# A fused attention and mixture-of-experts kernel: where the first silus and four halves of the shared expert stand at the end of the attention

## The chip, the cores and the metric

One Trainium2 chip, of which the kernel uses one core. The time is that of the program on the device, in microseconds. The kernel before was timed three times; their median counts. One more execution was taken by the hardware profiler, and all rows below come from it. TensorE is PE in the rows, VectorE DVE, ScalarE ACT, GpSimd POOL, SyncE SP.

## What is computed

Two layers over 2 x 2048 tokens of 256 channels, in float32:

```python
x = L0_attn_X
x = x + _L0_attn_ref(_layernorm(x), Wq, Wv, q_norm_w, v_norm_w)
x = x + _L0_ffn_ref(_layernorm(x), Wg, W1, W2, W3, Ws1, Ws2, Ws3)

# attention: no softmax, a running sum of outer products
K = X.reshape(B, L, H, d)                      # H = 16 heads of d = 16
Q = rms_norm_multihead((X @ Wq.T).reshape(B, L, H, d), q_norm_w)
V = rms_norm_multihead((X @ Wv.T).reshape(B, L, H, d), v_norm_w)
W = jnp.cumsum(jnp.einsum('blhd,blhde->blhde', K, V), axis=1)
out = jnp.einsum('blhd,blhde->blhe', Q, W)

# feed-forward: top 4 of 32 experts, and a shared expert of 256 hidden columns
scores = softmax(xf @ Wg); weights, indices = top_k(scores, 4)
y[tok] += (silu(xg @ W1[e]) * (xg @ W3[e]) @ W2[e]) * w     # for each expert e
z = silu(xf @ Ws1) * (xf @ Ws3) @ Ws2
return y + z
```

## The kernel before

The tokens are 32 tiles of 128 (NT = 32). Each engine has its own program, written out in Python and tied to the others by counting semaphores. Three stages follow each other:

1. The attention, with the routing woven in. `pipelined(NT, depth, step)` runs a step function that does parts of up to ten tiles in one step, each part for the tile `tile_of(skew)`. TensorE transposes, projects, makes the scores and the outputs; a tile's normalised second input (x2) is transposed 5 steps behind its first part and kept in x2T_all. Routing works on pairs of tiles (`closing(...)` is the second tile of a pair): router logits transposed (lgT, 5 steps behind), logits (6 behind, `pT0[:, P:P+2E]`, copied by ScalarE to lg), on VectorE the top four, the mask and the running count mcum, on TensorE the rank matmuls (7 behind, L846 and L847), copied by ScalarE to rk, and from it on VectorE the places posi. GpSimd scatters each tile's rows to the experts' table xs in memory by four indirect DMAs (L467).
2. Between attention and experts. TensorE counts the rows of each expert (L897), VectorE makes from it the table of 144 blocks (a chain of small operations, `tab(...)`, L1284 to L1329), TensorE turns two results into rows (L914, L916), VectorE writes them as brow and erow. SyncE waits for all scatters and for brow, then loads the blocks' rows into xg (L389).
3. The experts: 144 blocks of 128 rows. In a block TensorE transposes the rows (L946), ScalarE copies them (L647), TensorE multiplies by W1 and W3 (L967), ScalarE and VectorE do silu and product, TensorE multiplies by W2 (L985), ScalarE scales, GpSimd scatters to ys. After that the four parts of each token are summed and written out.

The shared expert is done in 8 groups g of 512 tokens. `shared_half(g, m, n)` is one of its four hidden halves (m: which 128 of 256 hidden columns; n = 0 the silu side, n = 1 the gate side), two matmuls of 128x512 (L741). `h_bank(g, m, n)` says in which PSUM bank it lies; banks come free from other work at different times, which sets the places of the halves. `half_silu(g, m)` (L624, ScalarE), `half_gate(g, m)` (L1249, VectorE: silu times gate side, into gsh), `shared_z(g)` (L757, TensorE: four output tiles, by turns in banks pQV and pO) and `add_z(t)` (L1259, VectorE, adds an output tile to x) make the rest. Groups 0 to 2 (NPRE = 3) are done before the blocks; five halves of groups 0 and 1 stand within the last steps of the attention, the others after them:

```python
if (a := closing(tile_of(7))) is not None:      # TensorE, the rank matmuls
    wait(pe, S["mask_done"], a.p + 1)
    wait(pe, S["mcum_done"], 2 * a.p + 1)
...
for q in range(QT):                             # TensorE, shared_z(g)
    wait(pe, S["z_done"], min(QT * g + q - 1, QT * LATE))
```

The last line is the one that ties an output tile to the adds: output q of a group waits until all but the one before it are added. VectorE's two gates of group 0 and the others of groups 0 and 1 stand at written places among the `tab(...)` operations, the four adds of group 0 behind L1317 among the last of them. Silu is in another table set of ScalarE than the exp and log of the attention, so `preload_act_table(ACT.Silu)` (L619) stands once, after the attention's last step. Of group 3 the two halves of m = 0 are done before and within the first block: H(3,0,0) ahead of the blocks, H(3,0,1) between the transposes of blocks 0 and 1; its silu and its product (kept) are done at block 1.

Of the kernel before, what the change touches and what calls it, by code (L numbers as in the profile page):

```python
# [12 lines left out]
ALU = mybir.AluOpType  # L13
ACT = mybir.ActivationFunctionType
# [37 lines left out]
def build(nc, X, Wq, Wv, q_norm_w, v_norm_w, Wg, W1, W2, W3, Ws1, Ws2, Ws3, out):  # L52
# [30 lines left out]
    ZC = 32  # L83
# [34 lines left out]
    with ctx:  # L118
# [386 lines left out]
        def _(act):  # L505
# [12 lines left out]

            normalise(0)
# [9 lines left out]
            def step(tile_of):  # L529
# [47 lines left out]
                if (a := closing(tile_of(7))) is not None:  # L577
                    wait(act, S["logits_ps"], a.p + 1)
                    wait(act, S["mask_done"], a.p - 1)
                    wait(act, S["max_done"], 2 * (a.p - 1))  # L580
                    act.copy(lg[:, a.pb].rearrange("p h e -> p (h e)"), pT0[:, P:P + 2 * E]).then_inc(S["lg_done"], 1)
                if (a := closing(tile_of(6))) is not None:
                    wait(act, S["lgT_ps"], a.p + 1)
                    wait(act, S["logits_ps"], a.p)
                    act.copy(lgT[:], pT0[:, 0:P]).then_inc(S["lgT_done"], 1)
                if (a := tile_of(0)) is not None and a.t > 1:
                    normalise(a.t)
# [33 lines left out]
            def half_silu(g, m):  # L621
                wait(act, S["h_ps"], FC * g + m + 1)
                wait(act, S["gsh_done"], FC * (g - 1) + m + 1)
                act.activation(sg[:, m, :], h_bank(g, m, 0)[:], ACT.Silu).then_inc(S["silu_done"], 1)  # L624

            def shared_silu(g):
                for m in range(FC):
                    half_silu(g, m)

            for g in range(NPRE):  # L630
                shared_silu(g)

# [8 lines left out]
            def expert_step(tile_of):  # L641
                if (a := tile_of(0)) is not None:
                    if a.t == 1:
                        half_silu(NPRE, 0)
                    wait(act, S["xT_ps"], a.t + 1)
                    wait(act, S["hb_ps"], a.t - 1)
                    act.copy(xgT[:, a.b], (pT0, pQV)[a.b][:, 0:D].rearrange("p (g m) -> p g m", g=KC)).then_inc(S["xT_done"], 1)  # L647
# [73 lines left out]
        def _(pe):  # L721
# [39 lines left out]
            def step(tile_of):  # L761
# [68 lines left out]
                if (a := closing(tile_of(6))) is not None:  # L830
                    if a.t == NT - 1:
                        pe.wait_ge(S["x2_done"], NT)
                        shared_half(1, 0, 1)
                    wait(pe, S["lgT_done"], a.p + 1)
                    wait(pe, S["x2T_done"], a.t + 2, NT)
                    wait(pe, S["qT_done"], a.t + 6, NT)
                    wait(pe, S["qm_done"], a.t + 6, NT)
                    pe.matmul(pT0[:, P:P + 2 * E], lgT[:], pick, start=True, stop=True).then_inc(S["logits_ps"], 1)
                if (a := closing(tile_of(7))) is not None:
# [54 lines left out]

            pe.wait_ge(S["mcum_done"], NT)
# [3 lines left out]
            pe.wait_ge(S["x2T_done"], NT)  # L899
            pe.wait_ge(S["silu_done"], 1)  # L900
            shared_half(1, 1, 1)
            pe.wait_ge(S["silu_done"], 2)
            shared_half(2, 0, 0)
            pe.wait_ge(S["gsh_done"], 1)
            shared_half(2, 0, 1)
# [34 lines left out]
            def expert_step(tile_of):  # L940
                if (a := tile_of(0)) is not None:
# [6 lines left out]
                    if a.t == 0:  # L948
                        shared_half(NPRE, 0, 1)
# [37 lines left out]
            shared_half(NPRE, 0, 0)  # L987
            pipelined(NJ, 4, expert_step)
# [20 lines left out]
        def _(dve):  # L1009
# [75 lines left out]

            def mask_scores(a, j):
                wait(dve, S["scores_ps"], 4 * a.t + j + 1)
                wait(dve, S["o_ps"], a.t)
                dve.tensor_tensor(s_sb[:, j].rearrange("p g r l -> p (g r) l"), pS[j][:].rearrange("p (n l) -> p n l", l=P),  # L1089
                                  tri[:].unsqueeze(1).to_broadcast([P, 4, P]), ALU.mult).then_inc(S["masked"], 1)  # L1090

            def step(tile_of):
# [21 lines left out]
                if (a := closing(tile_of(8))) is not None:  # L1114
# [4 lines left out]
                                      ).then_inc(S["mcum_done"], 1)  # L1119
                if (a := tile_of(3)) is not None:  # L1120
                    mask_scores(a, 3)
# [124 lines left out]
            def half_gate(g, m):  # L1246
                wait(dve, S["silu_done"], FC * g + m + 1)
                wait(dve, S["z_ps"], QT * (g - 1))
                dve.tensor_tensor(gsh[:, g % 2, m, :], sg[:, m, :], h_bank(g, m, 1)[:], ALU.mult).then_inc(S["gsh_done"], 1)  # L1249

            def shared_gate(g):
                for m in range(FC):
                    half_gate(g, m)

# [35 lines left out]
            dve.wait_ge(S["ys_zeroed"], 16 * ZC)  # L1290
            half_gate(0, 0)
            half_gate(0, 1)
# [7 lines left out]
            half_gate(1, 0)  # L1300
# [53 lines left out]
            shared_add(2)  # L1354
            dve.wait_ge(S["w2_in"], 16)

            def expert_step(tile_of):
# [4 lines left out]
                if (a := tile_of(0)) is not None:  # L1363
                    if a.t == 1:
                        dve.wait_ge(S["silu_done"], FC * NPRE + 1)
                        dve.tensor_tensor(sg[:, 0, :], sg[:, 0, :], h_bank(NPRE, 0, 1)[:], ALU.mult).then_inc(S["kept"], 1)
# [110 lines left out]
```

## Time and profile before

| | us |
|---|---|
| three runs | 560.71, 558.83, 557.15 |
| median | 558.83 |
| profiled execution | 559.33 |
| its span, first to last instruction | 557.4 |
| TensorE busy | 527.4 (95%) |
| VectorE busy | 382.2 (69%) |
| ScalarE busy | 376.5 (68%) |
| GpSimd busy | 331.8 (60%) |
| mean granted TensorE clock | 0.983 of full |

### The profile page before, as it was taken

What the parts mean: (1) busy time and instruction counts of PE and PEld (TensorE: products, weight loads), DVE (VectorE), ACT (ScalarE), POOL (GpSimd) and SP (SyncE); (2) the same over time, 40 slices, a digit from 0 to 9 for tenths busy, and PEclk for the clock granted to TensorE, in tenths of its full rate; (3) what the DMA queues carried; (4) which work ended last, traced back from release to release, by engine and by line L of the source; (5) the groups of instructions that cost most, each with busy time, mean ns of one, the idle gap of its engine ahead of it and who ended that gap; (6) DMA issues with size and microseconds to landing.
All of it is one profiled execution on the core that took longest, in us unless ns stands there. A gap on an engine that the chain in (4) does not pass through costs nothing.

```text
span 557.4 us, 18176 instructions
## 1 busy us (share of the span) xinstructions
PE 527.4 (95%) x5177; PEld 383.1 (69%) x5177; DVE 382.2 (69%) x1354; ACT 376.5 (68%) x1258; POOL 331.8 (60%) x367
## 2 busy tenths in 40 slices
PE   6798999999999999699999999999999999997996
PEld 2355666666666665357998988999999995544554
DVE  7698999999999996664444444444444446744786
ACT  2687899988989985402766766777677776653452
POOL 6010377776777777771665555666666564446992
PEclk8999999999999999899999999999999999998999
DMA  8998355556456554954676776766666554428999
GB/s 259 316 292 264 125 217 211 187 215 227 186 198 246 188 192 152 366 194 127 195 219 201 221 225 199 214 193 194 194 193 198 180 187 145 143 79 342 408 409 347
DMA packets 65088, 123.29 MB, mean 221 GB/s; under 512 B 9824, under 2 KB 44000, under 8 KB 64992
## 3 DMA queue, kind: packets, MB, share of 16 engines
q1 hardware_dynamic: 47824, 78.07, 44.1%
q0 software_dynamic: 13056, 39.86, 19.2%
q10 hardware_dynamic: 4112, 4.19, 2.3%
q8 instruction: 45, 0.74, 0.6%
q14 instruction: 51, 0.42, 0.3%
HBM read 58.49 MB, written 63.60 MB: 219 GB/s over the span
## 4 chain that ended last, share of the span: by engine, by line
PE 79%; DMA 5%; DVE 4%; issue 4%; ACT 3%; POOL 2%; SPq 1%; ACTq 1%; DVEq 0%; POOLq 0%
PE pS L967 18%; PE pQV L828 10%; PE pS L985 9%; PE pS L741 8%; PE pS L795 5%; PE pO L888 5%; DMA xg<-xs 3%; PE pO L869 3%; PE pT L946 3%; PE pQV L946 2%; PE pQV L757 2%; PE pO L757 2%; PE pT L774 2%; PE pO L803 2%; PE pT L817 1%
## 5 line engine op out<-in xcount | busy, mean ns | idle before, releaser
L495 POOL DMA_INDIRECT ys<-gsh,dst x144 | 138.1, 959 | 108.3 <-ACT gsh L663 86.6
L467 POOL DMA_INDIRECT xs<-xg,posi x128 | 123.8, 967 | 52.1 <-issue 31.4
L967 PE MATMUL pS<-after_a,x2T_all 128*128 128x128 f32 x1024 | 135.5, 276 | 0.0
L967 PEld LDWEIGHTS pS<-after_a,x2T_all 128*128 128x128 f32 x1024 | 124.5, 192 | 0.0
L1375 DVE TENSOR_TENSOR after_a<-after_a,pS 128x128 f32<-128x128 f32 x144 | 41.5, 288 | 79.9 <-ACT after_a L651 76.1
L1346 DVE COPY x2T_all<-w 128x512 f32 x144 | 63.9, 444 | 32.9 <-issue 32.5
L985 PE MATMUL pS<-w,after_a 128*128 x256 | 76.7, 381 | 0.0
L1089 DVE TENSOR_TENSOR w<-pS,tri 128x512 f32<-128x512 f32 x96 | 65.1, 679 | 1.0 <-PE pS L795 1.0
L828 PE MATMUL pQV<-w 128*128 128x512 f32 x128 | 63.7, 621 | 0.5 <-ACT w L533 0.5
L663 ACT ACTIVATE gsh<-pS,xg 128x256 f32<-128x256 f32 x128 | 60.6, 474 | 0.4 <-issue 0.4
L662 ACT CAST dst<-xg 128x1 int32 x128 | 24.5, 191 | 45.3 <-PE pS L985 43.3
L741 PE MATMUL pS<-x2T_all,ws 128*128 128x512 f32 x104 | 50.6, 636 | 1.3 <-ACT sg L624 0.7
L651 ACT ACTIVATE after_a<-pS 128x128 f32<-128x128 f32 x144 | 40.1, 279 | 16.5 <-PE pS L967 10.7
L482 POOL TENSOR_SCALAR_AFFINE_SELECT w<-w 128x512 f32<-128x512 f32 x32 | 20.6, 643 | 43.3 <-ACT w L527 43.0
L500 POOL TENSOR_TENSOR w<-w 128x512 f32<-128x512 f32 x32 | 40.7, 1272 | 7.7 <-DMA w<-ys 7.4
L985 PEld LDWEIGHTS pS<-w,after_a 128*128 128x128 f32 x256 | 38.9, 192 | 0.4 <-issue 0.4
L556 ACT ACTIVATE w<-pT,mwq 128x128 f32<-128x128 f32 x128 | 36.8, 379 | 1.9 <-PE pT L817 1.7
L741 PEld LDWEIGHTS pS<-x2T_all,ws 128*128 128x128 f32 x104 | 20.9, 207 | 24.6 <-issue 24.3
L795 PE MATMUL pS<-w 32*128 32x256 f32 x512 | 36.7, 401 | 0.0
L828 PEld LDWEIGHTS pQV<-w 128*128 128x128 f32 x128 | 22.2, 194 | 20.2 <-issue 18.2
L888 PE MATMUL pO<-w 128*32 128x128 f32 x1024 | 34.6, 274 | 1.3 <-POOL w L482 0.6
L647 ACT COPY after_a<-pT 128x256 f32<-128x256 f32 x72 | 26.1, 363 | 11.4 <-PE pT L946 11.3
(221 smaller groups left out, 1019.8 us busy)
## 6 DMA issues: line engine op xcount, KB each, us to landing
xg<-xs SPq DMA_DIRECT2D x128, 160.0 KB, 2.8
ys<-gsh SPq DMA_DIRECT2D x32, 512.0 KB
w<-ys SPq DMA_DIRECT2D x32, 512.0 KB, 15.3
w<-in_L_ffn_W ACTq DMA_DIRECT2D x1, 4096.0 KB, 18.6
out<-xall SPq DMA_DIRECT2D x14, 256.0 KB, 7.2
xs<-padrow SPq DMA_DIRECT2D x32, 80.0 KB
xg<-xs SPq DMA_DIRECT2D x32, 80.0 KB, 2.2
ys<-gsh,dst POOLq DMA_INDIRECT x144
```

Source lines behind the costliest of these rows:

```text
L467: pool.indirect_dma_start(out=xs, out_offset=bass.IndirectOffsetOnAxis(ap=posi[:, a.r8, k:k + 1], axis=0), in_=xr[:, a.r8, :], in_offset=N ...
L495: pool.indirect_dma_start(out=ys, out_offset=bass.IndirectOffsetOnAxis(ap=dst[:, j % 8:j % 8 + 1], axis=0), in_=y[:, j % 8, :], in_offset= ...
L663: act.activation(y[:, a.r8, :], pS[2 + a.b][:, 0:D], ACT.Copy, scale=xg[:, a.r8, bass.ds(e[0] + D, 1)]).then_inc(S["y_done"], 1)
L741: last = pe.matmul(h_bank(g, m, n)[:], ws13[:, k, n, m * P:(m + 1) * P], x2T_all[:, k, g * TG:(g + 1) * TG], start=(k == 0), stop=(k == KC ...
L795: last = pe.matmul(pS[j][:, g * 256:(g + 1) * 256], xnT[32 * j:32 * j + 32, a.r3, g, :], qm[32 * j:32 * j + 32, :, g, :], start=(g == 0), ...
L828: last = pe.matmul(pQV[:], xnT[:, a.r3, k, :], wqv[:, k, :], start=(k == 0), stop=(k == KC - 1))
L888: last = pe.matmul(pO[32 * j:32 * j + 32, g * P:(g + 1) * P], vp[:, a.b, 4 * g + j, r:r + 2, :], s_sb[:, j, g, r, :], start=False, stop=(r ...
L967: last = pe.matmul(pS[a.b][:, n * P:(n + 1) * P], w13_staged(a.t)[:, (2 * k + n) * F:(2 * k + n + 1) * F], xgT[:, a.b, k, :], start=(k == ...
L985: last = pe.matmul(pS[2 + a.b][:, 0:D], geT[:, a.b, :], w2_of(e), start=True, stop=True)
L1089: dve.tensor_tensor(s_sb[:, j].rearrange("p g r l -> p (g r) l"), pS[j][:].rearrange("p (n l) -> p n l", l=P), tri[:].unsqueeze(1).to_broa ...
L1346: dve.tensor_copy(w13_staged(j), w13[:, bass.ds(staged_of(j), 1), :, :, :].rearrange("p a k n f -> p (a k n f)")).then_inc(S["w13_staged"], 1)
L1375: dve.tensor_tensor((ge if mixed(a.t) else geT)[:, a.b, :], sge[:, a.b, :], pS[a.b][:, F:2 * F], ALU.mult).then_inc(S["ge_done"], 1)
```

## The change

Three things are moved; no computation is added or left out but two loads of activation tables.

- ScalarE loads the silu table behind the last lgT copy (step 6 behind, last tile), does both silus of group 0 there, goes on to the copy of the last logits, and loads the exp and log set again for what is left of the attention. The silu load after the attention stays.
- TensorE does H(1,1,1) and H(2,0,0) behind the last logits matmul and ahead of the last rank matmuls, and H(2,0,1) ahead of the count. VectorE does the two gates of group 0 behind its last first-half count (mcum), ahead of the rest of the last pair's routing, and the first gate of group 1 takes the old place of group 0's gates in the tables.
- Of group 3, H(3,0,1) follows H(3,0,0) ahead of block 0; its silu on ScalarE stands ahead of the blocks, its product on VectorE behind group 2's adds and ahead of the stage copy of block 1.

```diff
@@ ScalarE
                     act.copy(lg[:, a.pb].rearrange("p h e -> p (h e)"), pT0[:, P:P + 2 * E]).then_inc(S["lg_done"], 1)
+                    if a.t == NT - 1:
+                        act.preload_act_table_set("natural_log_exp_and_others")
                 if (a := closing(tile_of(6))) is not None:
                     ...
                     act.copy(lgT[:], pT0[:, 0:P]).then_inc(S["lgT_done"], 1)
+                    if a.t == NT - 1:
+                        act.preload_act_table(ACT.Silu)
+                        shared_silu(0)
...
             act.preload_act_table(ACT.Silu)
...
-            for g in range(NPRE):
+            for g in range(1, NPRE):
                 shared_silu(g)
+            half_silu(NPRE, 0)
...
                 if (a := tile_of(0)) is not None:
-                    if a.t == 1:
-                        half_silu(NPRE, 0)
@@ TensorE
                     pe.matmul(pT0[:, P:P + 2 * E], lgT[:], pick, start=True, stop=True).then_inc(S["logits_ps"], 1)
+                    if a.t == NT - 1:
+                        pe.wait_ge(S["x2T_done"], NT)
+                        pe.wait_ge(S["silu_done"], 1)
+                        shared_half(1, 1, 1)
+                        pe.wait_ge(S["silu_done"], 2)
+                        shared_half(2, 0, 0)
...
+            pe.wait_ge(S["gsh_done"], 1)
+            shared_half(2, 0, 1)
             pe.wait_ge(S["mcum_done"], NT)
             pe.wait_ge(S["rk_done"], NP2)
             pe.matmul(pT0[:, 0:E], ones16[:], mcum[:, 0, 0, :], start=True, stop=True).then_inc(S["cnt_ps"], 1)
-            pe.wait_ge(S["x2T_done"], NT)
-            pe.wait_ge(S["silu_done"], 1)
-            shared_half(1, 1, 1)
-            pe.wait_ge(S["silu_done"], 2)
-            shared_half(2, 0, 0)
-            pe.wait_ge(S["gsh_done"], 1)
-            shared_half(2, 0, 1)
...
-                    if a.t == 0:
-                        shared_half(NPRE, 0, 1)
...
             shared_half(NPRE, 0, 0)
+            shared_half(NPRE, 0, 1)
             pipelined(NJ, 4, expert_step)
@@ VectorE
                     dve.tensor_tensor(mcum[:, a.pb, 1, :], mcum[:, a.pb, 0, :], mask[:, a.pb, 0, :], ALU.add
                                       ).then_inc(S["mcum_done"], 1)
+                    if a.t == NT - 1:
+                        dve.wait_ge(S["ys_zeroed"], 16 * ZC)
+                        shared_gate(0)
...
-            dve.wait_ge(S["ys_zeroed"], 16 * ZC)
-            half_gate(0, 0)
-            half_gate(0, 1)
+            half_gate(1, 0)
...
-            half_gate(1, 0)
...
             shared_add(2)
+            dve.wait_ge(S["silu_done"], FC * NPRE + 1)
+            dve.tensor_tensor(sg[:, 0, :], sg[:, 0, :], h_bank(NPRE, 0, 1)[:], ALU.mult).then_inc(S["kept"], 1)
             dve.wait_ge(S["w2_in"], 16)
...
-                if (a := tile_of(0)) is not None:
-                    if a.t == 1:
-                        dve.wait_ge(S["silu_done"], FC * NPRE + 1)
-                        dve.tensor_tensor(sg[:, 0, :], sg[:, 0, :], h_bank(NPRE, 0, 1)[:], ALU.mult).then_inc(S["kept"], 1)
```

TensorE at the end of the attention before the change, from the last logits matmul on. L846 and L847 are the rank matmuls, L897 the count, L741 the halves by their banks (pS0 is H(1,1,1), pS2 H(2,0,0), pS1 H(2,0,1), pS3 H(2,1,0)), L757 the outputs of group 0:

```order
L838 MATMUL pT0<-after_a 128x64
L846 MATMUL pT0<-mask,tri16 128x64
L847 MATMUL pT0<-mcum,ones16 128x64
L897 MATMUL pT0<-mcum,ones16 128x32
L741 MATMUL pS0<-x2T_all,ws13 128x512 x2
L741 MATMUL pS2<-x2T_all,ws13 128x512 x2
L741 MATMUL pS1<-x2T_all,ws13 128x512 x2
L741 MATMUL pS3<-x2T_all,ws13 128x512 x2
L757 MATMUL pQV<-ws2,gsh 128x256 x2
L757 MATMUL pO<-ws2,gsh 128x256 x2
```

The same place after it (L842 is the last logits matmul, L856 and L857 rank, L909 the count, L745 the halves, L761 the outputs):

```order
L842 MATMUL pT0<-after_a 128x64
L745 MATMUL pS0<-x2T_all,ws13 128x512 x2
L745 MATMUL pS2<-x2T_all,ws13 128x512 x2
L856 MATMUL pT0<-mask,tri16 128x64
L857 MATMUL pT0<-mcum,ones16 128x64
L745 MATMUL pS1<-x2T_all,ws13 128x512 x2
L909 MATMUL pT0<-mcum,ones16 128x32
L745 MATMUL pS3<-x2T_all,ws13 128x512 x2
L761 MATMUL pQV<-ws2,gsh 128x256 x2
L761 MATMUL pO<-ws2,gsh 128x256 x2
```

Two halves now stand ahead of rank and a third ahead of the count. The order of all that follows the count is as it was.

VectorE where the tables begin, before the change: L1282 stands behind all routing, L1284 is the first operation that needs the count, L1249 are the two gates of group 0 (by their gate side's bank, pS1 and pS3):

```order
L1282 TENSOR_SCALAR padrow<-padrow 128x32
L1284 TENSOR_TENSOR pad_f<-pT0,ecap 128x32
L1285 CAST pad_i<-pad_f 128x32
L1286 TENSOR_TENSOR after_a<-pad_f,ebase 128x32
L1288 TENSOR_SCALAR after_a<-after_a 128x32
L1289 TENSOR_SCALAR after_a<-after_a 128x32
L1249 TENSOR_TENSOR gsh<-sg,pS1 128x512
L1249 TENSOR_TENSOR gsh<-sg,pS3 128x512
L1293 TENSOR_SCALAR after_a<-after_a 128x32
```

The same place after it (L1291 needs the count, L1093 with pO is the first gate of group 1):

```order
L1289 TENSOR_SCALAR padrow<-padrow 128x32
L1291 TENSOR_TENSOR pad_f<-pT0,ecap 128x32
L1292 CAST pad_i<-pad_f 128x32
L1293 TENSOR_TENSOR after_a<-pad_f,ebase 128x32
L1295 TENSOR_SCALAR after_a<-after_a 128x32
L1296 TENSOR_SCALAR after_a<-after_a 128x32
L1093 TENSOR_TENSOR gsh<-sg,pO 128x512
L1298 TENSOR_SCALAR after_a<-after_a 128x32
```

The gates of group 0 now come earlier, behind the last pair's first mcum (L1131), ahead of the reciprocal (L1154) and the rest of that pair's routing; one gate of group 1 has their place:

```order
L1131 TENSOR_TENSOR mcum<-mcum,mask 128x32
L1093 TENSOR_TENSOR gsh<-sg,pS1 128x512
L1093 TENSOR_TENSOR gsh<-sg,pS3 128x512
L1154 RECIPROCAL rin<-se 128x2
L1177 TENSOR_TENSOR vm<-mask,rk 128x64
```

They stood seven operations into the tables and stand before them now; the order of the tables themselves is unchanged.

## Rows read from the trace of the kernel before

**Rows 1.** The page's part 4, the chain that ended last: shares of the span.

```profile
PE 79%; DMA 5%; DVE 4%; issue 4%; ACT 3%; POOL 2%; SPq 1%; ACTq 1%; DVEq 0%; POOLq 0%
```

**Rows 2.** Timeline of TensorE: start, us, instruction, count, [idle before it <- what ended it].

```profile
227.96 0.33 PE L838 MATMUL pT<-after_a 128*128 128x64 f32 x2
...
230.11 0.19 PE L846 MATMUL pT<-mask,tri 128*128 128x64 f16 x1 [1.82 <-DVE mcum L1118]
...
231.74 0.21 PE L897 MATMUL pT<-mcum,ones 128*128 128x32 f16 x1 [1.41 <-DVE mcum L1096]
232.63 9.89 PE L741 MATMUL pS<-x2T_all,ws 128*128 128x512 f32 x16 [0.69 <-ACT sg L624]
242.36 1.03 PE L757 MATMUL pQV<-ws,gsh 128*128 128x256 f32 x4
...
245.81 1.88 PE L741 MATMUL pT<-x2T_all,ws 128*128 128x512 f32 x4
247.62 0.60 PE L914 MATMUL pT<-ident,ejc 128*1 128x128 f32 x4
...
251.09 1.13 PE L757 MATMUL pQV<-ws,gsh 128*128 128x256 f32 x4 [0.51 <-DVE xall L1259]
...
257.14 1.96 PE L741 MATMUL pS<-x2T_all,ws 128*128 128x512 f32 x4 [0.61 <-DVE xall L1259]
258.93 0.38 PE L946 MATMUL pT<-ident,xg 128*128 128x128 f32 x2
259.15 1.88 PE L741 MATMUL pS<-x2T_all,ws 128*128 128x512 f32 x4
...
261.09 1.06 PE L967 MATMUL pS<-after_a,x2T_all 128*128 128x128 f32 x8
```

**Rows 3.** Timeline of ScalarE, same columns.

```profile
226.43 0.27 ACT L585 COPY after_a<-pT 128x128 f32<-128x128 f32 x1
228.33 0.21 ACT L581 COPY lg<-pT 128x64 f32<-128x64 f32 x1 [1.63 <-PE pT L838]
...
230.59 1.28 ACT L619 ACT_TABLE_LOAD   x1
231.89 1.09 ACT L624 ACTIVATE sg<-pS 128x512 f32<-128x512 f32 x2
...
261.07 0.60 ACT L624 ACTIVATE sg<-pS 128x512 f32<-128x512 f32 x1 [1.29 <-PE pS L741]
261.56 0.37 ACT L647 COPY after_a<-pQV 128x256 f32<-128x256 f32 x1
```

**Rows 4.** Timeline of VectorE, same columns.

```profile
232.05 0.19 DVE L1284 TENSOR_TENSOR pad_f<-pT,ecap 128x32 f32<-128x32 f32 x1 [0.28 <-PE pT L897]
...
233.02 1.29 DVE L1249 TENSOR_TENSOR gsh<-sg,pS 128x512 f32<-128x512 f32 x2
...
240.50 0.36 DVE L1317 TENSOR_REDUCE stj<-after_a 128x2 f32<-128x196 f32 x1
243.49 0.42 DVE L1259 TENSOR_TENSOR xall<-xall,pQV 128x256 f32<-128x256 f32 x1 [2.63 <-PE pQV L757]
```

**Rows 5.** GpSimd's last scatter, SyncE's first loads of blocks, and issue to landing.

```profile
251.84 0.96 POOL L467 DMA_INDIRECT xs<-xg,posi  x1 [0.30 <-issue]
255.21 0.36 SPq L389 DMA_DIRECT2D xg<-xs  x1
256.06 0.34 SPq L389 DMA_DIRECT2D xg<-xs  x1
DMA to landing us min/median/max: 2.4/2.4/2.4
```

**Rows 6.** Busy time by engine in a stretch, then the mean granted clock (0.86).

```profile
230.00:232.00 2.00, 0.43 (x3) 0.23 (x3) 1.24 (x11) 1.61 (x3) 1.54 (x2) 0.86 1.05 392
```

**Rows 7.** The chain of waits late in the kernel, sixteen records of halves.

```profile
527.84 6.87 PE pS L741 x16
```

**Rows 8.** Timeline of TensorE at the start of the kernel.

```profile
10.35 3.27 PE L828 MATMUL pQV<-w 128*128 128x512 f32 x4 [0.46 <-ACT w L533]
```

More of the change, by code:

```diff
@@ L517, in normalise, with half_silu, shared_silu @@
                 act.activation(xn[:, t % 3, :], xall[:, t, :], ACT.Identity, bias=bias, scale=scale).then_inc(S["xn_done"], 1)
+            def half_silu(g, m):
+                wait(act, S["h_ps"], FC * g + m + 1)
+                wait(act, S["gsh_done"], FC * (g - 1) + m + 1)
+                act.activation(sg[:, m, :], h_bank(g, m, 0)[:], ACT.Silu).then_inc(S["silu_done"], 1)
+            def shared_silu(g):
+                for m in range(FC):
+                    half_silu(g, m)
             normalise(0)
@@ L619, in _ @@
             act.preload_act_table(ACT.Silu)
[L621 to L628, printed above, removed]
-            for g in range(NPRE):
+            for g in range(1, NPRE):
                 shared_silu(g)
+            half_silu(NPRE, 0)
             number = [[act.alloc_register(f"act_expert{h}_{n}") for n in range(4)] for h in range(2)]
@@ L1084, in _, with half_gate, shared_gate @@
             bias1(2)
+            def half_gate(g, m):
+                wait(dve, S["silu_done"], FC * g + m + 1)
+                wait(dve, S["z_ps"], QT * (g - 1))
+                dve.tensor_tensor(gsh[:, g % 2, m, :], sg[:, m, :], h_bank(g, m, 1)[:], ALU.mult).then_inc(S["gsh_done"], 1)
+            def shared_gate(g):
+                for m in range(FC):
+                    half_gate(g, m)
             def mask_scores(a, j):
@@ L1243, in _ @@
             pipelined(NT, 9, step)
[L1246 to L1253, printed above, removed]
             def add_z(t):
```

## The prediction

> I call the eight matmul groups of a shared-expert group g its halves, H(g,m,n): m is the half of the 256 hidden columns, n = 0 the silu side, n = 1 the gate side. Each is two matmul instructions, four records in the trace.
>
> **What bounds the kernel now.** I read the chain of waits first: TensorE holds 79% of it [rows 1], so what counts is when TensorE can go on. All edits lie between the last steps of the attention and the first matmul of routed block 0, so I then read TensorE's timeline there [rows 2]. The reader is to see four things in it. After the last logits matmul (L838, 227.96 + 0.33 = 228.29) TensorE has nothing for 1.82 us, does the rank matmuls, idles another 1.41 us, does the count (L897) and idles 0.69 us, until H(1,1,1) at 232.63. Then sixteen records of L741 take 9.89 us. The same sixteen take 6.87 us late in the kernel [rows 7]: 3.02 us are lost, since the granted clock fell in the idle stretch from the 2.4 GHz level to the 1.2 GHz one. Its mean of 0.86 over 230 to 232 us [rows 6] is 1.44 us at 1.0 and 0.56 us at 0.5, so it fell at 231.4. Last, block 0's first matmul (L967) starts at 261.09 with H(3,0,1) standing between the two transposes before it. From there on TensorE runs on without a gap, so I take the start of L967 as the measure of the whole change.
>
> Three other views say what may hold that start. ScalarE loads the silu table only at 230.59 and its first silu runs at 231.89 [rows 3]. VectorE makes the routing tables from 232.05 on (L1284) and is through the long part at 240.50 + 0.36 = 240.86 (L1317), then waits 2.63 us for the first shared output: TensorE is late here, not VectorE [rows 4]. And the block rows come from a scatter that GpSimd issues: its last scatter ends at 251.84 + 0.96 = 252.80, SyncE issues block 0's load at 255.21, and a load lands 2.4 us later, at 257.6 [rows 5]. The second is issued at 256.06 and lands at 258.5. Nothing in the diff touches GpSimd's order, and the last pair's places have slack: its eight scatters of 0.96 us begin before 245.1, while VectorE has the places done before its tables start at 232.05. So block 0's transposes can't start before 257.6, against 258.93 now.
>
> **The change, part by part.** I build the new timeline from the durations of the old one.
>
> *Silu early.* ScalarE is done with lgT (L585) at 226.70. The table load of 1.28 us and the first silu, 0.61 us until TensorE may use it, give 228.6; with the 0.14 us that TensorE took to react (232.63 against 231.89 + 0.60), H(1,1,1) starts at 228.74. The gap after L838 shrinks to 0.45 us. The two silus take 1.09 us, so the copy of the last logits (L581) runs at 229.0 instead of 228.33. That is 0.65 us, and it puts rank's inputs at 230.7.
>
> *Two halves ahead of rank.* A half costs 6.87/4 = 1.72 us. H(1,1,1) and H(2,0,0) run 228.74 to 232.18, so rank waits for them, not for its inputs: 232.2 instead of 230.11. H(2,0,1) stands before the count now: 232.25 to 233.97. The count was 1.63 us behind rank before (231.74 - 230.11), so it could run at 233.85; with the half it runs at 234.0. VectorE's tables then begin at 234.3 (0.31 us later, as before), 2.25 us later than now.
>
> *Two gates ahead of the tables.* Group 0's two gates, 1.29 us at 233.02 of now [rows 4], come before the tables, while VectorE would wait for rank: nothing is paid there. The tables from L1284 to the end of L1317 take 240.86 - 232.05 = 8.81 us, minus 1.29 = 7.5 us, so they end at 241.8.
>
> *The extra table loads on ScalarE.* Two more, 1.28 us each. The first is priced above. The load back to the exp set runs 229.2 to 230.5, ahead of three small activations and of the rank copy, which waits for TensorE until 232.4. The last silu load came 0.48 us after rank's start (230.59 against 230.11), so now at 232.7 to 234.0, and its silu is there at 234.6, ahead of the gate that takes it at 235.3. Both are hidden, the last with 0.7 us to spare; without that cover each costs 1.28 us.
>
> *What is late next.* After the count TensorE does H(2,1,0) to 235.75 and waits for group 1's first gate, at 234.3 + 0.97 = 235.3 on VectorE, done near 236.0. Two outputs of group 0 (0.86 us each: 245.81 - 242.36 is 3.45 for four) follow until 237.75. The third needs the bank that the first add frees, and this add stands behind the tables in VectorE's order: it starts at 241.8 and takes 0.42 us, and TensorE goes on at 242.3. **So an idle stretch of some 4.5 us opens on TensorE at 237.8, where there was none.** The tables were hidden behind TensorE's slow stretch; now they are the bound. From there: outputs three and four take 1.72 us, so H(2,1,1) starts at 244.0 and the row transposes (L914), 1.81 us later, at 245.8. VectorE's last table steps stand between its adds as now, and end ahead of them. The transposes start at 247.62 now: the gain here is 1.8 us; I carry 1.6, for waits between the many small steps. All up to H(3,0,0), with its waits for VectorE's adds, moves along: 257.14 becomes 255.5.
>
> *Group 3 ahead of block 0.* Both halves now run back to back, 255.5 to 259.1; the load has landed at 257.6. TensorE's work is the same, but the cover is gone: the silu of group 3 stands on ScalarE ahead of block 0's copy. It comes 1.92 us after the half starts (as 261.07 did after 259.15), the copy 0.49 us later (261.56 after 261.07, [rows 3]) and takes 0.37 us. The half starts at 257.35, so the copy ends at 260.13 and L967 starts at 260.2. VectorE's product of the same half and the stage copy of block 1 follow that silu; I count them as hidden behind the 0.9 us of block 0's matmuls and the transposes behind them, and block 1 slips by what sticks out. Without any change of clock the start is then 260.2 against 261.09: 0.9 us gained.
>
> *The clock.* The old stretch of idling that took the clock down had 3.1 us between 228.29 and the fall at 231.4, with two small matmuls in it. The new one is 4.5 us, empty, and the old one is gone. I expect the clock to fall in the new one. What that costs isn't in the old trace at this place, so I bound it: 3.02 us by the sixteen records at 232.63 [rows 2, 7], 1.4 us by the start of the kernel, where four records of this shape took 3.27 us after a gap [rows 8], against the 1.88 us of four at 245.81. Everything from 242.3 to the row transposes is TensorE-bound, so it's paid in full. I take the middle, 2.2 us, since the two rows are equally near.
>
> **Sum:** 559.33 (the profiled execution, 557.4 of span and 1.9 around it) - 0.9 + 2.2 = 560.6. It lies 0.5 us above the median of 558.83, so on the median's scale I forecast 558.8 + 1.3 = 560.1 us. The bounds of the clock give 559.3 to 560.9. A measurement can tell about 1% (5.6 us) from no change: this is no change.
>
> **The rivals.**
> *A, the clock stays up.* All as above, but TensorE idles at 237.8 without a fall. For it: the trace has one fall of this kind here, and what it hangs on besides the idling isn't seen in it. Against: the old, shorter idling did it. It gives 558.8 - 0.9 = 557.9.
> *B, the scatter is the bound.* If the tables end earlier than I add up (VectorE's chain is all small steps) and the idling is short, TensorE reaches block 0 before its rows. Transposes at 257.6 and 258.5, L967 at 258.8: 2.3 us gained, 556.5. It is the most that this change can win. Against: without a fall of the clock my sum has the transposes at 259.1, and it would take 1.5 us more that I don't find.
> *C, a table load costs more than its row.* The old load (L619) ends at 231.87 and the silu starts at 231.89, so no other cost shows behind it [rows 3]; what may lie ahead of it is at most the 0.48 us between rank's start and the load. Were the early load to cost its row twice, another 1.3 us, then H(1,1,1), rank, count and tables would all come 1.3 us later: 561.4.
> The Trainium skill, "ScalarE: Activation LUTs", section "What ACT_TABLE_LOAD costs", gives 1283 ns for the load and about 1380 ns for a drain with it. The row agrees with the first figure; a drain of that length has no room around it. By that page C would be the case, at nearly the same time; the trace speaks against it, and I leave it a small chance.
> *D, slower by much: the clock stays down up to the blocks.* Group 1's and 2's outputs are broken by waits (0.51 us at 251.09, 0.61 us at 257.14, [rows 2]). If these kept the clock at the low level from 242.3 on, the 15.9 us of TensorE's work between output three (242.36 + 1.72 = 244.1 now) and L967 at 261.09, less the two waits, would double: 558.8 - 0.9 + 15.9 = 573.8. It decides from some 7 us of half clock on. Against: the row of 9.89 us shows it back up after 3 us of lost time.
>
> **How the numbers follow.** Forecast 0.62, A 0.20, B 0.07, C 0.07, D 0.04. The range reaches down through A to near B, for the spread of the three runs too (557.15 to 560.71), and up beyond C: 557.0 to 562.0. Slower by over 1% is D, less a little: 0.03. Faster by over 1% would need 5.6 us where the scatter leaves 2.3, and gets 0.02 for what I don't see. The same: 0.95.
>
> **What would show it.** Right: H(1,1,1) near 228.7; the tables' first row near 234.3; an idle stretch of 4 to 5 us on TensorE after group 0's second output, ended by VectorE's add; a granted clock of 0.5 in and behind it and none near 232; the row transposes of L914 at 247 to 249. The start of block 0's first matmul within 260 to 263. Wrong: if the tables' first row comes before 233, if TensorE's idle time ahead of block 0 is ended by the load of xg (then B), or if the blocks behind it take another time than before.

## The result and the profile after

The changed kernel takes 561.89 us (median of 16 runs, 559.35 to 565.18), the kernel before 559.39 (16 runs, 557.10 to 561.45). The medians are 2.5 us apart. The ratio is 1.0037, 95% interval 1.0020 to 1.0054, and by it the change costs 2.1 us, 1.1 to 3.0 us: small, but "no change" lies outside the interval. The forecast was 1.3 us slower, and 560.1 us on the scale of the three first runs, whose median was 0.6 us lower.

| | before | after |
|---|---|---|
| profiled execution, us | 559.33 | 561.08 |
| span, us | 557.4 | 559.3 |
| TensorE busy, us | 527.4 | 528.6 |
| mean granted clock | 0.983 | 0.987 |

The two profiles don't enter the last steps of the attention at the same time: the last logits matmul starts at 227.96 before and at 227.38 after. I therefore measure each kernel by the **stretch** from the start of that matmul to the start of block 0's first one (L967 before, L970 now). It is 261.09 - 227.96 = 33.13 us before.

TensorE's timeline after, against [rows 2] (L842 the last logits matmul, L856 and L857 rank, L909 the count, L745 halves, L761 outputs, L919 row transposes, L970 the blocks' first matmuls; columns as there):

```profile
227.38 0.33 PE L842 MATMUL pT<-after_a 128*128 128x64 f32 x2
228.18 3.67 PE L745 MATMUL pS<-x2T_all,ws 128*128 128x512 f32 x8 [0.46 <-ACT sg L522]
231.68 0.19 PE L856 MATMUL pT<-mask,tri 128*128 128x64 f16 x1
...
233.54 0.18 PE L909 MATMUL pT<-mcum,ones 128*128 128x32 f16 x1
...
235.58 1.13 PE L761 MATMUL pQV<-ws,gsh 128*128 128x256 f32 x4
236.55 1.03 PE L761 MATMUL pO<-ws,gsh 128*128 128x256 f32 x4
242.03 2.07 PE L761 MATMUL pQV<-ws,gsh 128*128 128x256 f32 x4 [4.45 <-DVE xall L1266]
...
248.29 0.60 PE L919 MATMUL pT<-ident,ejc 128*1 128x128 f32 x4
...
257.81 3.67 PE L745 MATMUL pS<-x2T_all,ws 128*128 128x512 f32 x8 [0.61 <-DVE xall L1266]
...
262.52 1.13 PE L970 MATMUL pS<-after_a,x2T_all 128*128 128x128 f32 x8 [0.60 <-ACT after_a L651]
```

The reader is to see the three old gaps (1.82, 1.41 and 0.69 us) gone, one of 0.46 in their place, and a new one of 4.45 us behind group 0's second output, ended by VectorE's add. The stretch is 262.52 - 227.38 = 35.14 us: 2.0 us longer, as much as the spans of the two profiled executions differ (559.3 - 557.4 = 1.9). VectorE in the same stretch, against [rows 4]:

```profile
233.85 0.19 DVE L1291 TENSOR_TENSOR pad_f<-pT,ecap 128x32 f32<-128x32 f32 x1 [0.51 <-PE pT L909]
...
241.16 0.36 DVE L1321 TENSOR_REDUCE stj<-after_a 128x2 f32<-128x196 f32 x1
241.56 0.42 DVE L1266 TENSOR_TENSOR xall<-xall,pQV 128x256 f32<-128x256 f32 x1
```

The first add has no idle time before it now (2.63 us in [rows 4]): its output was there nearly 5 us earlier (235.58 + 1.13 = 236.71), and VectorE's own order held the add. ScalarE, against [rows 3]:

```profile
225.85 0.27 ACT L596 COPY after_a<-pT 128x128 f32<-128x128 f32 x1
226.14 1.28 ACT L598 ACT_TABLE_LOAD   x1
227.43 1.09 ACT L522 ACTIVATE sg<-pS 128x512 f32<-128x512 f32 x2
228.41 0.22 ACT L590 COPY lg<-pT 128x64 f32<-128x64 f32 x1
228.64 1.28 ACT L592 ACT_TABLE_LOAD   x1
229.94 0.20 ACT L611 ACTIVATE nmx<-m 128x2 f32<-128x2 f32 x1
...
232.17 1.28 ACT L633 ACT_TABLE_LOAD   x1
233.47 0.60 ACT L522 ACTIVATE sg<-pQV 128x512 f32<-128x512 f32 x1
```

Each load is 1.28 us, begins 0.01 to 0.02 us behind the copy ahead of it (the one of 232.17 stands behind a copy that ends at 232.15), and the next activation starts 0.01 to 0.02 us behind it. The granted clock, third from the end of a row, against [rows 6]:

```profile
230.00:232.00 2.00, 2.00 (x8) 0.95 (x7) 1.44 (x4) 0.92 (x6) 1.52 (x2) 1.00 1.05 395
...
240.00:242.00 2.00, 0.00 (x0) 0.00 (x0) 1.82 (x7) 0.00 (x0) 1.70 (x2) 0.63 0.45 164
242.00:244.00 2.00, 1.97 (x5) 1.61 (x6) 0.88 (x5) 0.00 (x0) 1.39 (x3) 0.50 0.35 124
244.00:246.00 2.00, 2.00 (x6) 1.58 (x5) 0.73 (x4) 0.00 (x0) 1.51 (x2) 0.50 0.34 126
246.00:248.00 2.00, 2.00 (x4) 0.55 (x2) 1.17 (x4) 0.00 (x0) 1.57 (x2) 0.66 0.46 162
```

The clock no longer falls at 231 us. It falls within the new idle stretch (a mean of 0.63 over 240 to 242 us puts the fall at 240.5, 2.9 us after TensorE's last matmul), stays at the 1.2 GHz level for all of 242 to 246 us, and is up again in 246 to 248.

### The profile page after: what moved, and what is told of

It reads as the page before. It is cut to its first block, busy times and chain, and to the rows that moved or that the text cites. A ratio compares the mean times of both kernels' runs of the same rounds, so it can differ in the third digit from the quotient of the medians.

```text
span 559.3 us, 18178 instructions
## 1 busy us (share of the span) xinstructions
PE 528.6 (95%) x5177; PEld 382.9 (68%) x5177; DVE 382.5 (68%) x1354; ACT 378.1 (68%) x1260; POOL 332.8 (59%) x367
## 4 chain that ended last, share of the span: by engine, by line
PE 74%; DVE 6%; SPq 5%; issue 4%; DMA 4%; POOL 2%; ACT 2%; ACTq 0%; DVEq 0%; POOLq 0%
PE pS L970 17%; PE pQV L832 10%; PE pS L988 8%; PE pS L745 7%; PE pS L799 5%; PE pO L898 5%; DMA xg<-xs 3%; PE pO L879 3%; PE pQV L761 2%; PE pT L951 2%; SPq L384 2%; PE pQV L951 2%; PE pO L761 2%; PE pT L778 2%; PE pO L807 2%
## 5 line engine op out<-in xcount | busy, mean ns | idle before, releaser
L970 PE MATMUL pS<-after_a,x2T_all 128*128 128x128 f32 x1024 | 135.5, 275 | 0.7 <-ACT after_a L651 0.6
L970 PEld LDWEIGHTS pS<-after_a,x2T_all 128*128 128x128 f32 x1024 | 124.4, 192 | 1.2 <-issue 1.1
L832 PE MATMUL pQV<-w 128*128 128x512 f32 x128 | 62.3, 609 | 0.5 <-ACT w L542 0.5
L745 PE MATMUL pS<-x2T_all,ws 128*128 128x512 f32 x104 | 48.1, 610 | 1.1 <-DVE xall L1266 0.6
L745 PEld LDWEIGHTS pS<-x2T_all,ws 128*128 128x128 f32 x104 | 19.7, 196 | 22.6 <-issue 22.2
L951 PE MATMUL pT<-ident,xg 128*128 128x128 f32 x144 | 28.1, 277 | 2.5 <-DMA xg<-xs 2.1
```

Source lines behind the costliest of these rows:

```text
L745: last = pe.matmul(h_bank(g, m, n)[:], ws13[:, k, n, m * P:(m + 1) * P], x2T_all[:, k, g * TG:(g + 1) * TG], start=(k == 0), stop=(k == KC ...
L832: last = pe.matmul(pQV[:], xnT[:, a.r3, k, :], wqv[:, k, :], start=(k == 0), stop=(k == KC - 1))
L951: last = pe.transpose((pT0, pQV)[a.b][:, g * P:(g + 1) * P], xg[:, a.r8, g * P:(g + 1) * P], ident[:])
L970: last = pe.matmul(pS[a.b][:, n * P:(n + 1) * P], w13_staged(a.t)[:, (2 * k + n) * F:(2 * k + n + 1) * F], xgT[:, a.b, k, :], start=(k == ...
```

## The experiments

Twelve runs. Theory 1 is that of the prediction: the new idle stretch takes the clock down, and that costs more than the early silus bring. Ratios are to the kernel before, timed on the same chip beside them. Each stretch is that of one profiled execution; the times are medians of six to twelve where nothing else is said.

### Throwaway matmuls in the new idle stretch

```diff
+            def fill(times, first, width):
+                for _ in range(times):
+                    pe.matmul(pT0[:, first:first + width], w_bd[:, 0, 0:P], w_bd[:].rearrange("p b c -> p (b c)")[:, 0:width],
+                              start=True, stop=True, skip_group_check=True)
...
                 for q in range(QT):
+                    if g == 0 and q == 2:
+                        fill(10, D, 256)
```

> The changed kernel, with ten throwaway matmuls of 128x256 (0.43 us each at full clock, 4.3 us in all) put where TensorE idles 4.45 us, between group 0's second and third output. They write a part of bank pT0 that nobody reads. Theory 1 (the fall of the clock in the idle stretch makes the loss): the stretch fills, the granted clock stays at 1.0, the eight matmuls of outputs three, four and H(2,1,1) up to L919 take about 3.5 us instead of 6.26, and block 0's first matmul starts 2.7 us earlier against the same start of the last steps: 0.995 of the changed kernel, 0.998 to 1.000 of the kernel before. Rival (the loss comes from group 3's halves and silu ahead of block 0, or from the two table loads): no gain, still 1.003 to 1.005 of the kernel before.

557.82 us against 559.16: 0.9967 (0.9944 to 0.9989). TensorE:

```profile
228.64 0.33 PE L849 MATMUL pT<-after_a 128*128 128x64 f32 x2
...
238.66 4.48 PE L733 MATMUL pT<-w_bd 128*128 128x256 f32 x20
243.27 1.13 PE L768 MATMUL pQV<-ws,gsh 128*128 128x256 f32 x4
...
246.91 0.60 PE L926 MATMUL pT<-ident,ejc 128*1 128x128 f32 x4
...
261.14 1.13 PE L977 MATMUL pS<-after_a,x2T_all 128*128 128x128 f32 x8 [0.60 <-ACT after_a L651]
```

From output three to the row transposes it is 3.64 us here and 6.26 us (242.03 to 248.29) in the changed kernel: the fall of the clock costs 2.6 us. The stretch is 32.50 us, 0.6 us shorter than before and 2.6 us shorter than the changed kernel's. TensorE does more work here and is done earlier. The rival, for which filling the gap would gain nothing, falls. The gain in time is larger than was expected (0.998 to 1.000). It isn't that of the profiled execution alone: the mean granted clock of the whole kernel has a median of 0.9925 over the twelve executions, against 0.987 over the 35 of the kernel before and 0.986 over the sixteen of the changed one.

### The same in the kernel before

```diff
                     pe.matmul(pT0[:, P:P + 2 * E], lgT[:], pick, start=True, stop=True).then_inc(S["logits_ps"], 1)
+                    if a.t == NT - 1:
+                        pe.wait_ge(S["lg_done"], NP2)
+                        fill(6, 3 * P, P)
...
+            pe.wait_ge(S["rk_done"], NP2)
+            fill(4, 3 * P, P)
             pe.wait_ge(S["mcum_done"], NT)
```

> The kernel before, with throwaway matmuls (128x128 into an unused part of pT0, six behind the last logits copy, four behind the last rank copy) in the idle stretch that takes its clock down at 231.4 us. Nothing is moved. Theory 1: the sixteen records behind 232.6 take 6.9 us instead of 9.9, the tables (end of L1317 near 240.9) then hold output three, the row transposes start 2.7 us earlier, and the landing of block 0's rows becomes the bound ahead of the blocks: TensorE idles over 1 us there, block 0's first matmul starts 1.3 us earlier, 0.997 to 0.999 of before. Rival (the clock costs nothing, since something else is as late): 1.000.

557.60 us against 559.16: 0.9964 (0.9940 to 0.9987).

```profile
227.03 0.33 PE L843 MATMUL pT<-after_a 128*128 128x64 f32 x2
...
231.70 7.10 PE L746 MATMUL pS<-x2T_all,ws 128*128 128x512 f32 x16 [0.71 <-ACT sg L624]
...
256.61 0.44 PE L956 MATMUL pT<-ident,xg 128*128 128x128 f32 x2 [1.01 <-DMA xg<-xs]
...
258.82 1.06 PE L977 MATMUL pS<-after_a,x2T_all 128*128 128x128 f32 x8
```

The sixteen records take 7.10 us instead of 9.89, 2.8 us less, and ahead of block 0 TensorE now waits 1.01 us for the rows, the bound that the prediction named as rival B. The stretch is 31.79 us, 1.3 us shorter, as expected (the ratio is a little better than the 0.997 to 0.999 expected). So 1.5 of the 2.8 us are lost again, 1.0 of them in the wait for the rows. The median of the mean granted clock is 0.9945. With ten throwaway matmuls and nothing moved, the old order does better than the changed kernel as it stands (0.9964 against 1.0037), and is not to be told by time from the changed kernel with its gap filled (0.9967).

### Only the third edit

The kernel before, with H(3,0,1), its silu and its product ahead of the blocks, as in the diff of the change.

> The kernel before with only the third edit: H(3,0,1) behind H(3,0,0), its silu and its product ahead of the blocks. Theory 1: TensorE's work is the same, but it waits 0.4 to 0.7 us for ScalarE ahead of block 0's first matmul (the silu stands ahead of the copy): block 0's first matmul starts 0.4 to 0.7 us later, 1.001 of before. Rival (this edit makes the loss): 1.003 to 1.004 of before.

560.05 us against 559.16: 1.0016 (0.9997 to 1.0035).

```profile
228.59 0.33 PE L837 MATMUL pT<-after_a 128*128 128x64 f32 x2
...
257.62 3.67 PE L740 MATMUL pS<-x2T_all,ws 128*128 128x512 f32 x8 [0.60 <-DVE xall L1257]
...
262.34 1.13 PE L964 MATMUL pS<-after_a,x2T_all 128*128 128x128 f32 x8 [0.60 <-ACT after_a L646]
```

The stretch is 33.75 us, 0.6 us longer, and the 0.60 us stand in the row. From H(3,0,0) to block 0's first matmul it is 4.72 us, against 3.95 before (261.09 - 257.14): here the edit costs 0.8 us, of which 0.2 us don't show in the stretch, since the sixteen records took 9.72 us in this execution and not 9.89. By time alone the interval doesn't exclude no change.

### Only the first two edits

The changed kernel with H(3,0,1), its silu and its product back in blocks 0 and 1.

> The changed kernel without the third edit: silus, halves and gates of group 0 early, group 3 as before. Theory 1: the idle stretch of 4.5 us and the fall of the clock are here, and the row transposes start about 1.2 us later than before; 1.002 to 1.003 of before. Rival (group 3's edit makes the loss): 0.997 to 0.999, the 1.6 us that the silus gain.

560.74 us against 559.16: 1.0024 (1.0000 to 1.0047).

```profile
228.68 0.33 PE L843 MATMUL pT<-after_a 128*128 128x64 f32 x2
...
243.30 2.08 PE L762 MATMUL pQV<-ws,gsh 128*128 128x256 f32 x4 [4.45 <-DVE xall L1268]
...
263.12 1.06 PE L973 MATMUL pS<-after_a,x2T_all 128*128 128x128 f32 x8
```

The same idle stretch of 4.45 us; the stretch as a whole is 34.44 us, 1.3 us longer. With the 0.6 us of the third edit that makes 1.9, against 2.0 for the whole change. The interval begins at no change (1.0000), so by time alone this one too is barely told.

### Four runs on another chip

The next four ran on a chip on which the kernel before takes 708.14 us. ScalarE is idle there for up to 12.4 us at a time, for a reason that the profile names only as "remote"; the cause is open, and these ratios are not set beside the others. The changed kernel itself wasn't run there, so what its variants gain over it on that chip isn't known.

```profile
331.83 0.21 ACT L585 COPY rk<-pT 128x64 f32<-128x64 f32 x1 [12.40 <-remote]
```

> The changed kernel, with VectorE's four adds of group 0 moved forward into the tables (the first two behind the first scans, the third behind group 1's second gate, the fourth behind the first reduce), where the outputs are ready. Nothing is added. Theory 1 (the first add's place behind the tables opens the idle stretch): outputs three and four follow without the 4.45 us, TensorE idles instead 2 to 3 us for the last table step, the row transposes start 3.5 to 4 us earlier than in the changed kernel, and the landing of block 0's rows becomes the bound. Block 0's first matmul near 259.0 to 259.5 us: 0.996 to 0.997 of before. If the clock falls in the shorter stretch, 1 to 2 us of that are lost. Rival (the tables' own start is what is late, whatever the adds do): 1.002.

VectorE's four `add_z` calls of group 0 moved forward: 702.81 us, 0.9921 (0.9892 to 0.9950).

> The changed kernel, with group 3's silu on ScalarE behind block 0's copy instead of ahead of it. Theory 1: the 0.60 us that TensorE waits for that copy ahead of block 0's first matmul shrinks to 0.3 to 0.4 us; 0.2 to 0.3 us gained, not to be told from the changed kernel by time: 1.003 of before. Rival (the silu in that place costs more than its wait): 1.000 to 1.001.

`half_silu(NPRE, 0)` behind the first block's copy: 702.23 us, 0.9928 (0.9901 to 0.9955). TensorE's wait ahead of block 0's first matmul is 0.39 us instead of 0.60, as expected. The second half of the trade shows one block on: block 1's first matmul starts 1.46 us behind block 0's (357.87 to 359.33) instead of 1.18 (262.52 to 263.70), since its own copy now stands behind the silu. What the time of this edit alone would be on the other chips wasn't tried.

> Both of the above: the adds of group 0 early and group 3's silu behind block 0's copy. Theory 1: TensorE has done group 3's halves before the rows land, so the silu is out of the way in any case; block 0's first matmul at 259.0 to 259.3 us, held by the landing of the rows, as with the adds alone: 0.996 of before. Rival (the silu still counts): 0.3 us better than the adds alone.

Both: 702.75 us, 0.9923 (0.9895 to 0.9951). The three can't be told from each other there, and the numbers expected of them in us and ratios don't hold on that chip.

> The early silus without group 3's edit once more, for a second look at where the clock falls: an idle stretch of 4.4 to 4.6 us behind group 0's second output again, and a fall of the clock within it or up to 1 us behind it; the eight matmuls of outputs three, four and H(2,1,1) take between 4.9 and 6.6 us. Rival (the fall is chance): 3.5 us in this run.

700.80 us, a single execution. The stall of ScalarE holds rank's copy back and TensorE idles 11.90 us ahead of the count; the idle stretch behind group 0's second output is 2.96 us, not 4.4 to 4.6, and outputs three, four and H(2,1,1) run at full clock behind it (341.90 to 345.62, 3.72 us). The expectation missed, and the 3.72 us are near the 3.5 of its rival (the fall is chance), though behind a shorter stretch than it speaks of. This chip's order of waits is another one, so the run says nothing of how often a stretch of 4.45 us takes the clock down.

### The changed kernel again, and the adds moved

These two ran on another chip again, on which the kernel before takes 559.76 us. The diff leaves out the lines that take the adds from their old places.

```diff
             tab(dve.tensor_scalar(ends[:, 1, E:E + 1], ends[:, 1, E:E + 1], float(2 * NU), None, ALU.max))
+            add_z(0)
...
             tab(dve.tensor_tensor(cst[:, 0, 0:E], n64[:, 0], ends[:, 0, 0:E], ALU.subtract))
+            add_z(1)
...
             half_gate(1, 1)
+            add_z(2)
...
             tab(dve.tensor_reduce(ej[:], behind[:], AX_X, ALU.add))
+            add_z(3)
```

> The changed kernel unaltered, beside the two variants with VectorE's adds moved, since the first runs of these were on a chip on which the kernel before takes 708 us. 1.003 to 1.005 of before; if this call's chip is again such a one, all ratios may differ, and only the order within the call counts.

> As the first run of this kernel was to show: the changed kernel with VectorE's four adds of group 0 forward in the tables. Theory 1: 0.996 to 0.997 of before, 0.993 of the changed kernel, no idle stretch over 3 us on TensorE between the logits and block 0, block 0's transposes held by the landing of the rows. Rival (the tables' own start is what is late): 1.002 of before.

The changed kernel: 561.23 us against 559.76, 1.0044 (1.0022 to 1.0066). With the adds moved: 559.98 us, 0.9992 (0.9967 to 1.0016), less of a gain than the 0.996 to 0.997 expected.

```profile
228.11 0.33 PE L842 MATMUL pT<-after_a 128*128 128x64 f32 x2
...
238.83 1.13 PE L761 MATMUL pQV<-ws,gsh 128*128 128x256 f32 x4 [0.47 <-DVE xall L1266]
...
245.17 1.01 PE L919 MATMUL pT<-ident,ejc 128*1 128x128 f32 x4 [2.61 <-DVE ejc L1333]
...
255.78 3.67 PE L745 MATMUL pS<-x2T_all,ws 128*128 128x512 f32 x8 [0.60 <-DVE xall L1266]
...
260.49 1.13 PE L970 MATMUL pS<-after_a,x2T_all 128*128 128x128 f32 x8 [0.19 <-ACT after_a L651]
```

The 4.45 us are gone, 0.47 us stand there; instead TensorE waits 2.61 us for the last table step, and the clock falls even in this shorter stretch:

```profile
244.00:246.00 2.00, 0.83 (x5) 0.49 (x6) 1.55 (x7) 0.00 (x0) 1.43 (x2) 0.70 0.33 123
246.00:248.00 2.00, 2.00 (x8) 1.22 (x7) 0.92 (x3) 0.00 (x0) 1.45 (x2) 0.50 0.34 123
```

The stretch is 32.38 us, 0.75 us shorter than before. The place of the first add is what opened the long gap; the tables, by their own start and length, leave a shorter one.

### The adds, the copy and four throwaway matmuls

Both kernels have the adds moved and `half_silu(NPRE, 0)` behind the first block's copy; the first also has `fill(4, D, 256)` ahead of TensorE's wait for `tab_blk`.

> The changed kernel with VectorE's adds of group 0 moved forward, group 3's silu behind block 0's copy, and four throwaway matmuls (1.7 us, bank pT0) in the 2.6 us that TensorE now waits for the last table step. Theory 1: the granted clock stays at 1.0 between the attention and the blocks, the row transposes start about 2.9 us after H(2,1,1) ends minus nothing for half clock, and block 0's transposes wait for the landing of the rows; block 0's first matmul 1.5 to 2.5 us earlier than in the kernel before: 0.995 to 0.998 of it, with 0.9965 the likeliest. Rival (what is gained ahead of the blocks is lost in them): 1.000.

> The same without the throwaway matmuls. Theory 1: TensorE idles 2.6 us for the last table step and the clock falls there in some executions, as it did with the adds moved alone (0.9992 of before). 0.997 to 1.000 of before, 0.5 to 1.5 us above the kernel with the throwaway matmuls. Rival (the clock has no part in it): the same time as that one.

These two ran on yet another chip, on which the kernel before takes 559.65 us. With the throwaway matmuls it is 558.81 us: 0.9980 (0.9959 to 1.0000). Without them it is 558.96 us: 0.9981 (0.9959 to 1.0002). First the rows with them:

```profile
227.35 0.33 PE L848 MATMUL pT<-after_a 128*128 128x64 f32 x2
...
244.45 0.60 PE L926 MATMUL pT<-ident,ejc 128*1 128x128 f32 x4 [0.89 <-DVE ejc L1340]
...
258.46 1.13 PE L977 MATMUL pS<-after_a,x2T_all 128*128 128x128 f32 x8 [0.32 <-ACT after_a L650]
```

The stretch is 31.11 us, 2.0 us shorter than before, and without the throwaway matmuls it is as short, 258.43 - 227.35 = 31.08 us, since in that profile the clock stayed up through the same 2.61 us idle:

```profile
227.35 0.33 PE L843 MATMUL pT<-after_a 128*128 128x64 f32 x2
...
244.41 0.60 PE L920 MATMUL pT<-ident,ejc 128*1 128x128 f32 x4 [2.61 <-DVE ejc L1334]
...
253.93 3.67 PE L746 MATMUL pS<-x2T_all,ws 128*128 128x512 f32 x8 [0.60 <-DVE xall L1267]
...
258.43 1.13 PE L971 MATMUL pS<-after_a,x2T_all 128*128 128x128 f32 x8 [0.23 <-ACT after_a L650]
```

```profile
242.00:244.00 2.00, 0.00 (x0) 0.00 (x0) 1.73 (x10) 0.44 (x1) 1.46 (x2) 1.00 0.37 136
244.00:246.00 2.00, 1.59 (x11) 1.16 (x12) 1.44 (x5) 0.00 (x0) 1.43 (x2) 1.00 0.30 110
```

So the expected 0.5 to 1.5 us between these two isn't seen; the medians are 0.15 us apart. Both lie below the kernel before by 0.7 to 0.8 us in the medians, at the edge of what twelve executions of each can tell.

These rows price the fall behind the shorter idle stretch. From the row transposes to H(3,0,0) it is 253.93 - 244.41 = 9.52 us with the clock up, and 255.78 - 245.17 = 10.61 us with the adds moved alone, where it fell: 1.1 us. They also show that placing group 3's silu behind the first copy gains nothing. From H(3,0,0) to block 0's first matmul it is 4.50 us instead of 4.71 (260.49 - 255.78), but to block 2's first matmul 7.61 us (261.54 - 253.93) instead of 7.44 (263.22 - 255.78). The changed kernel has 4.71 and 7.44 too. What the stretch shows as gained is lost, and 0.2 us more, behind its end.

| kernel | stretch, us | against 33.13 | ratio of times |
|---|---|---|---|
| changed (first profile) | 35.14 | +2.0 | 1.0037 |
| changed, again | 34.97 | +1.8 | 1.0044 |
| only edits one and two | 34.44 | +1.3 | 1.0024 |
| only edit three | 33.75 | +0.6 | 1.0016 |
| changed, gap filled | 32.50 | -0.6 | 0.9967 |
| changed, adds early | 32.38 | -0.75 | 0.9992 |
| before, gaps filled | 31.79 | -1.3 | 0.9964 |
| adds early, copy first, filled | 31.11 | -2.0 | 0.9980 |
| adds early, copy first | 31.08 | -2.05 | 0.9981 |

Stretches and ratios don't fall in one order: -2.0 us goes with 0.9980 and -0.6 us with 0.9967. The last two kernels give 0.4 us back in the blocks: block 2's first matmul starts 3.11 us behind block 0's, against 2.72 in the kernel before (263.81 - 261.09). And each stretch shows the clock of one execution: the profiled one of the kernel with the adds, the copy and the throwaway matmuls had a mean granted clock of 0.996, the highest of its twelve, whose median is 0.9885. The stretch tells where a change acts; by time the kernels from 0.9964 to 0.9981 can't be told from each other.

## Why the prediction was right, and where it was off

The forecast was right in its mechanism, and its two terms of size were each a little off.

*Silu early* held: H(1,1,1) starts 0.80 us behind the logits matmul's start (228.18 - 227.38; forecast 0.78), gap 0.46 (0.45).

*Two halves ahead of rank* held: rank 4.30 us behind the logits matmul (forecast 232.2 - 227.96 = 4.24), the tables' start 6.47 us behind it (6.34).

*The table loads* held: each 1.28 us with nothing around it, so rival C didn't come. The drain of about 1380 ns that the Trainium skill ("ScalarE: Activation LUTs", "What ACT_TABLE_LOAD costs") puts with a load is not in these rows. The silu behind the last load was done at 234.07 and its gate starts at 234.84, 0.8 us later (forecast 0.7).

*What is late next* held, and it is the step on which all rests: 4.45 us idle (forecast 4.5), ended by the first add behind the tables. That moving the adds leaves 0.47 us of this gap shows the cause.

*Group 3 ahead of block 0* held: the forecast had 260.2 - 255.5 = 4.7 us from H(3,0,0) to the block's first matmul, against 3.95 before. Measured is 262.52 - 257.81 = 4.7 us, and 4.7 us too with this edit alone, so its price is 0.8 us as forecast.

*No clock change* was to bring 0.9 us; with the gap filled 0.6 us is measured. Of the 1.6 us carried for the row transposes 1.4 are there: they start 246.91 - 228.64 = 18.27 us behind the logits matmul, against 247.62 - 227.96 = 19.66 before. Less the 0.8 us of group 3 that leaves the 0.6.

*The clock* is the term that was mis-sized: 2.2 us taken, 2.6 measured, inside the bounds of 1.4 and 3.0. The middle was a choice between two rows, not a derivation; the nearer one was the sixteen records at the same place, whose fall was read at 3.02 us and cost 2.8 by the run that filled the old gaps. The two errors, 0.3 us without the clock and 0.4 with it, point the same way and add up. Together -0.6 + 2.6 = +2.0 us against the forecast +1.3. Of the 1.8 us between 560.1 and the measured 561.89, 0.6 lie in the scale: three runs of before had given 558.83, sixteen gave 559.39. So 561.89 lies inside the stated range of 557.0 to 562.0 only just. The prediction took 1% as the least that can be told; sixteen executions of each told 0.37%.

Rival A didn't come: in neither profile of the changed kernel did the clock stay up, nor in that of the first two edits alone. Rival B's bound is real, and was reached in another order (1.01 us of waiting for the rows with the old gaps filled). Rival D didn't come: the mean of 0.66 over 246 to 248 us puts its return at 247.4, 5.3 us after TensorE went on.

One count ahead of the prediction is wrong, without touching it: not five but seven halves of groups 0 and 1 stand within the last steps of the attention before the change, and H(1,1,1) is the eighth.

## What to carry to other kernels

A wait that vanishes lets the next in line decide: here VectorE's table chain, hidden until then behind TensorE's slow stretch, with an add at its end that a PSUM bank hung on. Before moving work forward on one engine, look at where the other engine's small releasing operation stands in its order. And where a stretch of TensorE's idling can't be closed, count the half clock behind it as well as the idling: it cost 2.6 us after 4.45 us here, and ten throwaway matmuls took it away. The price of a fall already stood in the old trace, at the fall that the change was to remove. And a stretch that ends too early counts as gained what the next block pays: take its end where the blocks follow each other at the old distance again.

## What the runs showed of the hardware

The same idle stretch of 2.61 us took the clock down in one profile (0.70, then 0.50) and left it at 1.00 in another, with nearly the same work around it but on two chips; whether the chip decides isn't shown. In the kernel before it fell at 231.4, within the second of two idle times of 1.82 and 1.41 us that have two small matmuls between them. A fall behind a stretch of that length isn't something to count on either way. Ten small matmuls that compute nothing, put into the 3.9 us of gaps of the kernel before, gained 0.36% (0.13 to 0.60%).

Late in the kernel the clock falls too, and not always. The mean over 500 to 552 us is 0.93 in the profile of before and 1.00 in that of the changed kernel with its gap filled, although nothing in their code differs there. The row of before comes first:

```profile
500.00:552.00 52.00, 47.66 (x140) 27.43 (x138) 36.02 (x88) 22.74 (x41) 40.67 (x32) 0.93 0.97 375
```

And that of the changed kernel with its gap filled:

```profile
500.00:552.00 52.00, 44.77 (x141) 25.79 (x139) 38.48 (x93) 22.89 (x40) 40.61 (x32) 1.00 1.01 392
```

This may be one source of the spread of 4 us and more between runs of one kernel (it wasn't tried), and is a reason to read where 1 to 2 us come from in the stretch, and not from single times. Last, one chip took some 27% longer for the kernel before (708.14 against 559.16 us) and 26% longer with the adds moved (702.81 against 559.98), with idle times of ScalarE up to 12.40 us that the profile names only as "remote".
